# A two-layer attention and mixture-of-experts kernel: where routing is woven into the expert tiles, and how the tiles' rows reach the tensor engine

## The reference

```
x = x + attn_a(layernorm(x))   # one head, rotary tables
x = x + ffn(layernorm(x))      # 8 experts, each row goes to one
x = x + attn_b(layernorm(x))   # 16 heads of 64, causal
x = x + ffn(layernorm(x))      # the same experts again
```

## Time and profile before

| | |
|---|---|
| median of three runs | 843.16 us (843.04 to 843.72) |
| the profiled execution's own time | 842.97 us |
| its span, first to last instruction | 841.1 us |
| mean granted clock of the tensor engine | 0.991 of full |
| PE / PEld / DVE / ACT / POOL busy | 95% / 82% / 74% / 67% / 52% |

### The profile page before, as it was taken

How to read it: one execution, slowest core, us unless ns; L and a number is a source line. 1 busy time by engine, 2 the same in 40 slices (tenths; PEclk the granted TensorE clock), 3 DMA queues, 4 the chain that set the end, 5 groups by cost and what they waited for, 6 DMA issues and landing times.

```text
span 841.1 us, 22553 instructions
## 1 busy us (share of the span) xinstructions
PE 800.6 (95%) x6857; PEld 692.8 (82%) x6860; DVE 620.5 (74%) x2697; ACT 562.0 (67%) x2028; POOL 433.6 (52%) x755
## 2 busy tenths in 40 slices
PE   8999879999899999999999999999999999899993
PEld 5887749999788888888888888888778888589992
DVE  4889766666667777777877777887767776676765
ACT  2666636666777777777777777777767777356661
POOL 3343737775544544544444444444874544247772
PEclk9999999999999999999999999999999999999997
DMA  9940021431200000000000000000020000003135
GB/s 323 337 132 2 23 89 47 132 96 39 74 2 2 2 2 2 2 2 1 2 2 1 3 2 2 2 2 2 31 95 3 2 2 2 2 23 125 54 102 168
DMA packets 27702, 40.65 MB, mean 48 GB/s; under 512 B 4672, under 2 KB 19904, under 8 KB 26560
## 3 DMA queue, kind: packets, MB, share of 16 engines
q1 hardware_dynamic: 20480, 27.91, 10.3%
q0 software_dynamic: 4992, 10.27, 3.7%
q10 hardware_dynamic: 2112, 1.05, 0.5%
HBM read 20.79 MB, written 18.43 MB: 47 GB/s over the span
## 4 chain that ended last, share of the span: by engine, by line
PE 74%; DVE 10%; POOL 7%; issue 6%; DMA 2%; ACT 1%; DVEq 1%; SPq 0%; POOLq 0%
PE PS L1205 11%; PE PS L1217 10%; PE PS L1196 10%; PE PS L1169 9%; PE PS L1160 9%; PE PS L1248 6%; PE PS L1040 5%; PE PS L1042 5%; PE PS L1041 5%; POOL xs_dram L333 2%; POOL w1b L366 2%; PE PS L1152 1%; POOL pb L392 1%; POOL rstdA L328 1%; POOL pb L390 1%
## 5 line engine op out<-in xcount | busy, mean ns | idle before, releaser
L390 POOL TENSOR_SCALAR pb<-pb,rib 128x128 f32<-128x128 f32 x256 | 95.3, 372 | 251.7 <-DVE rib L920 251.0
L911 DVE CUSTOM_DVE_ANT_0 PS<-PS,CST 128x128 f32<-128x128 f32 (+1 forms) x512 | 169.0, 383 | 60.7 <-PE PS L1217 60.5
L925 DVE COPY pT<-PS 128x384 f32<-128x384 f32 x256 | 140.3, 555 | 37.5 <-PE PS L1196 37.0
L526 ACT ACTIVATE pb<-PS,nbb 128x128 f32<-128x128 f32 x256 | 94.9, 371 | 96.5 <-DVE nbb L911 92.7
L499 ACT ACTIVATE yT<-PS,w1b 128x128 f32<-128x128 f32 x368 | 104.9, 368 | 61.5 <-PE PS L1160 61.5
L392 POOL TENSOR_SCALAR pb<-pb,rib 128x256 f32<-128x256 f32 x256 | 122.3, 478 | 0.0
L1196 PE MATMUL PS<-CST,pb 128*128 128x128 f32 x768 | 117.7, 279 | 4.1 <-POOL pb L392 3.6
L528 ACT ACTIVATE pb<-PS,nbb 128x256 f32<-128x256 f32 x256 | 121.2, 473 | 0.0
L349 POOL DMA_INDIRECT yt_dram<-XY x92 | 92.1, 1001 | 35.9 <-issue 21.9
L1196 PEld LDWEIGHTS PS<-CST,pb 128*128 128x128 f32 x768 | 85.8, 142 | 27.9 <-issue 23.2
L1205 PE MATMUL PS<-pT,vb 128*64 128x256 f32 (+1 forms) x1024 | 103.3, 339 | 2.2 <-DVE pT L925 1.8
(11 more groups left out here) (132 smaller groups left out, 1682.4 us busy)
## 6 DMA issues: line engine op xcount, KB each, us to landing
xs_dram<-XY SPq DMA_DIRECT2D x2, 1483.5 KB, 15.7
XY<-xs_dram SPq DMA_DIRECT2D x2, 1225.5 KB, 6.1
W1S<-in_W SPq DMA_DIRECT2D x1, 2048.0 KB, 20.8
W2S<-in_W SPq DMA_DIRECT2D x4, 512.0 KB, 8.2
xs_dram<-XY SPq DMA_DIRECT2D x1, 1612.5 KB, 10.9
out_dram<-X SPq DMA_DIRECT2D x6, 256.0 KB, 2.4
yt_dram<-XY POOLq DMA_INDIRECT x92, 2.6
xs_dram<-XY SPq DMA_DIRECT2D x1, 1354.5 KB, 11.9
```

Of the source, the lines that this page charges most:

```text
L390: nc.gpsimd.tensor_scalar(pb[:, i, 0:P], pb[:, i, 0:P], rib[:, i, 0:1], 1.0, ALU.mult, ALU.mult)
L911: last = nc.vector.tensor_tensor_reduce(ps, ps, CST[:, m:m + c1 - c0], -SCALE_B, HIGHEST, ALU.add, ALU.min, nbb[:, hh % 4, c0 // P:c0 // P ...
L925: nc.vector.tensor_copy(pT[:, hh % 4, :], PS[:, bank, 0:3 * P]).then_inc(b_pT, 1)
```

## The change

1. Layer one: DVE runs eight operations of `route(1)` ahead instead of 18, and weaves the other 20 into steps 0 to 4. The fillers ahead of step 0 are 6 instead of 20.
2. Layer two: PE, ACT and DVE carry out steps 0 to 3 of the experts before or inside the last step of attention b. On DVE, steps 0 and 1 stand in the middle of step 17, step 2 behind it, step 3 in the middle of step 18. On PE and ACT steps 0 to 3 stand between steps 17 and 18. Routing of the last group is woven into steps 4 to 10. PE's `route(3)` stands behind its step 5. The fillers of this stretch are gone. ACT loads Gelu's table ahead of step 0.
3. The two operations that make the last group's gates go to the very end (`gates(3)`), and ACT's exponentials for them behind the last step; so POOL waits for 26 operations there.
4. PE transposes the rows straight out of `XY`; the buffer `xs1`, DVE's copies and `f_in` are gone. PE waits for the loads itself, and POOL's pace counts `f_xT_ps`, the transposes, from one tile earlier.
5. The loads have three parts: tiles 0 and 1, 2 to 7, the rest.
6. The last batch's router uses another PSUM bank.

```diff
-XCHUNKS = ((0, 4), (4, None))
+XCHUNKS = ((0, 2), (2, 8), (8, None))
...
+def once_bank(b):
+
+    return T_BANK if b == NB - 1 else ONCE_BANK
...
             def before_scatters(k):
-                pool.wait_ge(r_step, STEPS * (k + 1))
+
+                pool.wait_ge(r_step, STEPS * (k + 1) - (2 if k == 3 else 0))
...
-                pool.wait_ge(f_in, NL + SCATTER_PACE[1][t])
+                pool.wait_ge(f_xT_ps, NL + SCATTER_PACE[1][t])
                 scatter(3, t)
...
# ACT
-                route(GROUPS * layer + 1)
-                load_table(ACT.Gelu)
-                expert_steps(step, 0, first_quarter if layer == 0 else None)
+                if layer == 0:
+                    route(1)
+                    load_table(ACT.Gelu)
+                    expert_steps(step, 0, first_quarter)
+                else:
+
+                    load_table(ACT.Gelu)
+                    for s in range(4):
+                        step(s, s % RING)
+                    attn_b(NB + 2, 0)
+                    expert_steps(step, 4)
+                    route(3)
...
# DVE
-                dve.wait_ge(r_exp, k + 1)
-                yield from then(nc.vector.reduce_sum(den, ex, AX.X))
-                yield from then(nc.vector.reciprocal(GATE[:, t0:t0 + gt], den))
+                if k < 3:
+                    yield from gates(k, done)
...
-                    j = s
-                    if has(j, NL):
-                        for kk in range(GROUPS):
-                            for c, (j0, _) in enumerate(XCHUNKS):
-                                if fixed(j) and j == (NJS[GROUPS * layer] if kk else j0):
-                                    dve.wait_ge(xs_in[GROUPS * layer + kk][c], 16)
-                        wait(dve, f_xT_ps, ring(j))
-                        nc.vector.tensor_copy(xs1[:, w, :], XY[:, ds(j), 0:D]).then_inc(f_in, 1)
...
+                if layer == 0:
+                    for _ in range(AHEAD):
+                        next(parts)
+                    first, woven = 0, -((AHEAD - STEPS) // 4)
+                else:
+
+                    routing, parts = parts, iter(())
+                    step(0, 0)
+                    step(1, 1)
+                    attn_b(NB + 1, 1, 2, QUADS)
+                    step(2, 2)
+                    attn_b(NB + 2, 0, 0, 2)
+                    step(3, 3)
+                    attn_b(NB + 2, 0, 2, QUADS)
+                    parts = routing
+                    first, woven = 4, 4 + -((2 - STEPS) // 4)
+                for s in range(first, woven):
                     step(s, s % RING)
                 for _ in parts:
                     pass
                 expert_steps(step, woven, first_quarter if layer == 0 else None)
+                if layer == 1:
+                    for _ in gates(3):
+                        pass
...
-            peeled(attn_b, ROUTE2_AT + 3, 19)
+            peeled(attn_b, ROUTE2_AT + 3, NB + 1)
+            attn_b(NB + 1, 1, 0, 2)
             experts(1)
...
# PE
-                        pe.wait_ge(f_in, n + 1)
+                        for kk in range(GROUPS):
+                            for c, (j0, _) in enumerate(XCHUNKS):
+                                if j == (NJS[GROUPS * layer] if kk else j0):
+                                    pe.wait_ge(xs_in[GROUPS * layer + kk][c], 16)
                         wait(pe, f_xT, ring(j))
-                        tr(PS[:, 2 + v, 0:P], xs1[:, v, :], ident).then_inc(f_xT_ps, 1)
+                        tr(PS[:, 2 + v, 0:P], XY[:, j, 0:D], ident).then_inc(f_xT_ps, 1)
...
-                route(GROUPS * layer + 1)
-                keep_clock((20, 0)[layer], 4)
-                step(0, 0)
-                step(1, 1)
-                step(2, 2)
-                keep_clock((6, 10)[layer], 4)
-                expert_steps(step, 3, first_quarter if layer == 0 else None)
+                if layer == 0:
+                    route(1)
+                    keep_clock(6, 4)
+                    step(0, 0)
+                    step(1, 1)
+                    step(2, 2)
+                    keep_clock(6, 4)
+                    expert_steps(step, 3, first_quarter)
+                else:
+
+                    for s in range(4):
+                        step(s, s % RING)
+                    attn_b(NB + 2, 0)
+                    step(4, 0)
+                    step(5, 1)
+                    route(3)
+                    expert_steps(step, 6)
...
-                        if fixed(s) and s >= NB + 1:
-                            keep_clock((11, 10)[s - (NB + 1)], T_BANK)
...
-AHEAD = (18, 0)
-
-SCATTER_PACE = (tuple(2 + 3 * t // 4 for t in range(GTS[1])), tuple(7 + 3 * t // 4 for t in range(GTS[3])))
+AHEAD = 8
+
+SCATTER_PACE = (tuple(1 + 3 * t // 4 for t in range(GTS[1])), tuple(6 + 3 * t // 4 for t in range(GTS[3])))
```

More of the change, by code:

```diff
@@ L243, in build @@
         returned, lent_returned = [sem(f"returned{k}") for k in range(4)], sem("lent_returned")
-        f_in, f_xT_ps, f_xT, f_w, f_h_ps, f_gelu, f_y_ps, f_y = (
-            sem("f_" + n) for n in ("in", "xT_ps", "xT", "w", "h_ps", "gelu", "y_ps", "y"))
+        f_xT_ps, f_xT, f_w, f_h_ps, f_gelu, f_y_ps, f_y = (
+            sem("f_" + n) for n in ("xT_ps", "xT", "w", "h_ps", "gelu", "y_ps", "y"))
         b_wh, b_wl = (sem(n) for n in ("b_wh", "b_wl"))
@@ L378, in _ @@
             for t in range(GTS[1]):
-                pool.wait_ge(f_in, SCATTER_PACE[0][t])
+                pool.wait_ge(f_xT_ps, SCATTER_PACE[0][t])
                 scatter(1, t)
@@ L584, in _ @@
             attn_b(ROUTE2_AT, ROUTE2_AT % 2, 1, QUADS)
-            peeled(attn_b, ROUTE2_AT + 1, 19)
+            peeled(attn_b, ROUTE2_AT + 1, NB + 2)
             experts(1)
@@ L737, in attn_a, with gates @@
                 part()
+            def gates(k, done=None):
+                t0, gt = GT0[k], GTS[k]
+                done = done or [STEPS * (k + 1) - 2]
+                dve.wait_ge(r_exp, k + 1)
+                for what in range(2):
+                    if what == 0:
+                        last = nc.vector.reduce_sum(r_den[:, 0:gt], r_ex[:, 0:gt, :], AX.X)
+                    else:
+                        last = nc.vector.reciprocal(GATE[:, t0:t0 + gt], r_den[:, 0:gt])
+                    done[0] += 1
+                    last.then_inc(r_step, 1)
+                    yield
+                    dve.wait_ge(r_step, done[0])
             def route(k):
@@ L813, in route @@
                 yield from then(nc.vector.tensor_scalar(TE[:, NJ0[k]:NJ0[k] + nj], te, float(E - 1), None, ALU.min))
-                assert done[0] == STEPS * (k + 1), done[0]
+                assert done[0] == STEPS * (k + 1) - (2 if k == 3 else 0), done[0]
             def experts(layer):
@@ L855, in step @@
                     part()
-                    j = s
-                    if has(j, NL):
-                        for kk in range(GROUPS):
-                            for c, (j0, _) in enumerate(XCHUNKS):
-                                if fixed(j) and j == (NJS[GROUPS * layer] if kk else j0):
-                                    dve.wait_ge(xs_in[GROUPS * layer + kk][c], 16)
-                        wait(dve, f_xT_ps, ring(j))
-                        nc.vector.tensor_copy(xs1[:, w, :], XY[:, ds(j), 0:D]).then_inc(f_in, 1)
-                for _ in range(AHEAD[layer]):
-                    next(parts)
-                woven = -((AHEAD[layer] - STEPS) // 4)
-                for s in range(woven):
+                if layer == 0:
[14 more added lines that the diff above has]
+                for s in range(first, woven):
                     step(s, s % RING)
@@ L977, in attn_b @@
                     if q == 2 and has(gb):
-                        logits(gb + NB, TPB * gb, ONCE_BANK)
+                        logits(gb + NB, TPB * gb, once_bank(gb))
                     if q == 3 and has(s):
@@ L1273, in attn_b @@
                         wait(pe, r_lg, gb + NB)
-                        router_T(gb + NB, ONCE_BANK)
+                        router_T(gb + NB, once_bank(gb))
                     if q == 2 and has(gb):
-                        router(gb + NB, v, ONCE_BANK)
-                        if fixed(s) and s >= NB + 1:
-                            keep_clock((11, 10)[s - (NB + 1)], T_BANK)
+                        router(gb + NB, v, once_bank(gb))
                     if q == 3 and has(s):
```

5 lines of the change are left out of this document (2 added, 3 removed).

## The result

The changed kernel takes 847.01 us (median of 5 runs, 846.08 to 850.48), the kernel before in the same comparison 843.08 (5 runs, 842.95 to 843.72): a ratio of 1.0048, 95% interval 1.0031 to 1.0065. It is slower by 3.9 us, where 2.9 us less was forecast. I therefore count each stage from its own start.

What follows compares the result with a forecast made beforehand. The prediction took PE's tile starts to bound layer one and POOL's give-back queue layer two's end. From 843.16 us, -2.6 (layer one), -0.6 (layer two) and +0.3 (clock) gave 840.3 us, range 837.0 to 843.2.

Steps and rivals of the forecast that it cites:

- Layer one's gain: Layer one's start: fewer routing operations ahead bring tile 2's product at 128.8 instead of 131.43, 2.6 us gained.
- That cover: Layer one: scatters and load are through at about 158, before tile 21 needs them at 161.1; some 3 us spare.
- Layer two's routing: Attention b's end: first routing operation 1.4 us later, first scatter 2.3 us later, at 748.4.
- the clock's: Both layers' starts: PE's clock may fall, costing at most 1.7 us of work each, at least nothing; 0.3 taken.
- Rows 8: Profile rows, end of attention a: PE busy 2.27 of 4 us, granted clock fell from 2.4 to 1.2 GHz.
- The rows for tile 23: Layer two, last group: load and scatter latencies of 2.5 us put rows at 773.6, just when PE wants them; no cost.
- the overlap taken for free: Layer two, tile 23: a stall for rows would only use time for which tiles wait for POOL anyway.
- POOL's pace: Layer two's give-backs: 1.267 us each up to the last, unchanged by removing one of three DVE copies per tile.
- the first rival: Layer two: POOL keeps up, so the tiles' lead reaches the end; 836.4, or about 838.5 if half holds; chance 0.16.
- The sum: Whole kernel: -2.6 layer one, -0.6 layer two, +0.3 clock, together -2.9 us.
- The fourth: Rival, last group: half clock slows three woven routing steps, POOL starts 4.8 us later still; 846.2; chance 0.08.
- the second: Rival, both thin stretches: half clock takes 1.4 in layer one, delays layer two's routing 1.0; 842.4; chance 0.19.

Runs made afterwards that it cites:

- e1: Changed kernel with fillers added where PE idles at both layers' starts, nothing else; 845.27 us, ratio 1.0025.
- e3: Kernel before with layer one's part alone: eight routing operations ahead, 6 fillers; 841.43 us, ratio 0.9979.
- e9: Changed kernel with fillers added at both starts and PE waiting for the second group's three loads one by one; 839.92 us, ratio 0.996.
- e10: e9 with ACT's last router copy ahead of tile 0's Gelu and eight of layer two's routing operations run ahead; 837.89 us, ratio 0.9936.
- e11: Changed kernel with PE waiting for the second group's three loads one by one, no fillers added; 844.36 us, ratio 1.0012.
- e2: Kernel before with only its fillers cut to the change's (6 ahead of layer one's step 0, none in layer two); 845.87 us, ratio 1.0031.
- e12: e10 without the fillers added in layer one; 838.86 us, ratio 0.9951.
- e5: Same program as e9, run on another chip where the kernel before took 892.47 us; 891.82 us, ratio 0.9991.

## Why the prediction was wrong

**Layer one's gain** was mis-sized: 2.6 forecast, 2.05 with the clock held (e1, e3, e9, e10), 0.93 in the profile of after. The first difference, 0.6, lies in the chain of DVE that I had added up: in e1 tile 2's weights are there 128.86 - 116.64 = 12.22 us behind the routing's first operation, and in after as much, where my 128.7 is 11.65. I had taken 0.47 for the gap at each register load, and two of the three gaps on that way are longer. In after:

```profile
125.43 0.31 DVE L825 TENSOR_TENSOR r_exc<-r_ps,r_exc 128x144 f32<-128x144 f32 x1 [0.63 <-DVE r_exc L822]
...
129.87 0.37 DVE L837 TENSOR_TENSOR r_cmp<-CST,r_cum 128x200 f32<-128x200 f32 x1 [0.84 <-DVE POS L833]
```

For e1 the profile puts the end of PE's wait at tile 2 down to a copy by ACT that ends at 128.96, but by the kernel's order that copy is of tile 3's rows; the weights, there 0.11 before the product, are what was missing. The second difference is the clock. The first scatter of the group comes at 131.60 - 1.97 = 129.63, 2.8 later than before, where I had 2.3. That cover held in after: PE does not stop in layer one there. In e1 it failed by 1.40, because PE waited for all three loads; in e9, with the waits one by one, it held.

**Layer two's routing** was right in its sum and wrong in its condition. I put the first scatter at 748.4; with the clock held it is 748.46. That it fits so well is luck in part: the first routing operation comes 6.73 - 4.96 = 1.77 us later instead of 1.4, and from it to the first scatter e1 takes 0.57 longer instead of 0.9. In after the first scatter comes at 752.55 - 0.83 = 751.72 in the same frame. The step that failed is the clock's: "In layer one it would shift every tile; in layer two mostly hide behind DVE and POOL. I take 0.3". It does not hide behind DVE, since DVE's waits for PE grow with it (1.33 us for the router product, 0.73 for a tile's product, 1.21 for the counts), nor behind POOL, whose queue bounds the end from its first scatter on. The cost was 3.3 us. Rows 8 had shown a clock that fell after 2.27 busy of 4 us; I expected some 2 busy of 4 and still leaned towards nothing.

**The rows for tile 23.** "No cost, but no room; a stall there would only use time for which the tiles have to wait for POOL anyway." Both halves are wrong. I had priced the first of the three loads, and PE's code waits at that tile for all three. SP issues them from 774.66. Their sizes and times to landing in this stretch of after:

```profile
XY<-xs_dram SPq DMA_DIRECT2D x1, 967.5 KB, 6.5
XY<-xs_dram SPq DMA_DIRECT2D x1, 387.0 KB, 3.9
...
XY<-xs_dram SPq DMA_DIRECT2D x1, 129.0 KB, 2.1
```

The first, estimated at 2.5, lands in 2.1 and would have been there at 776.8, before PE wanted it at 782.22 - 4.35 = 777.87. The third lands 6.5 us behind its issue. And the spare time was smaller than the stall: by my working the tiles were ready by 822.6 and POOL came at 826.8, 4.2 us; the stop of 4.35 and 2.6 lost at half clock behind it (782.22 to 788.66 for two tiles of 1.90) together take 7. e9 and e11 show what is left without it: a queue of 78.65, where I had worked out 826.8 - 748.4 = 78.4. This is the second step that failed, the overlap taken for free: e11 against after puts its price at 2.65 us.

**POOL's pace** was right within about 1%: in e9 the first give-back starts at 768.87 and the last at 826.46, 57.59 / 45 = 1.280 us each, where I took 1.267. With one DVE copy in each tile fewer it did not quicken; over the same first 37 intervals it is 1.267 before and 1.284 in e9. The Trainium skill's page "SBUF — State Buffer", section "Who interferes with whom", would have had POOL quicken; by its rule the first rival would have come, and these traces don't show it.

**The sum** against the profiles. Routing 3.3, queue 81.77 - 78.4 = 3.4, layer one 13.45 - 11.75 = 1.7: 8.4 us. The forecast and the measured median, 840.3 and 847.01, differ by 6.7. The profiled execution of after is the slowest of its five and stands 3.5 above their median. Of this, 0.5 lies outside its span (850.48 - 848.0 against 847.01 - 845.0) and up to 1.97 ahead of the change. The profile's distances hold 1.7 us more than the medians differ by, and how the median run splits its loss no profile shows.

**The rivals.** The fourth came true in its sign: its point of decision was a first scatter 5 us late, and it came 5.6 late. That its time, 846.2, lies only 0.8 under the median is luck. It asked for 4.8 us in three slow steps on top of the forecast's delay, and the half clock cost 3.3, of which 1.33 came ahead of the routing, at the router product. It had no stop at tile 23. e11 is its case without that stop, 844.36. I gave it 0.08, because I thought that a PE with a backlog keeps its clock. Its clock did not return through 4 us at full use (736 to 740). Rows 8 should have made the half clock the likely case in both thin stretches, and the second and the fourth rival should have held most of the chance. The forecast's own order of work was sound: e9, the same weaving with clock and waits held up, comes to -3.05 us where -2.9 was forecast. By the distances it comes to -2.05 - 0.32 = -2.4, so a part of that agreement is chance as well.

The page "TensorE: Matmul & The Clock Gate" of the Trainium skill says, in its part on the HAM clock gate, that the default state is throttled and activity releases it, and in "HAM oscillation — how this bites in real kernels" that a wait for a DMA between bursts of products leaves the next burst at the low clock. The stop of 4.35 us and the 1.93 us behind it, for a product that takes 1.06 at full clock, agree with that. The falls in the two starts came without such a wait: PE's longest single wait ahead of them was 2.03 us, and it ended at DVE's weight copy.

## What to carry to other kernels

Work that looks idle may hold a clock: when a change removes fillers, price the half clock as the likely case, and along every chain in which another engine waits for TensorE's small products. When a load is cut into parts, check where the consumer waits for each: a part brings nothing while one tile waits for all. And when one queue bounds the end, what counts is when it starts and whether anything makes it wait; the kernel gained 5.1 us once its start, the clock and the waits were put right together. A sum that agrees is no proof of its terms: here the fourth rival's time agreed with the median although one of its terms was too large and the stop was not in it.

## What the hardware showed that I had not expected

A fall of the clock can outlast the thin stretch by much. In after it lasted from about 730 to 740, with PE busy for 2.93 and then 4.00 of 4 us. In e2 it also lasted some 10 us, there with PE busy for 1.29 and 2.30 of 4 us and only then for all of its time (740 to 742, granted clock 0.53).

The same program in the same stretch does not always lose it. Over 124 to 128 in layer one PE was busy for 2.21 of 4 us in e11 and 2.14 in e12, and the granted clock was 0.76 in the one and 1.00 in the other. Whether kernels with thin stretches spread more is not shown: e11 went from 841.95 to 847.29 in 12 runs, and the kernel before beside it from 842.56 to 846.16 in 17.

One chip ran the kernel before in 892.47 us instead of 843. In e5's profile there attention took as long as elsewhere, and the experts did not. What stops the engines there no run here shows.
